# One GRU's gates, blend and norm scale split into pieces and dealt out over attention tiles

## The reference

```
x = x + gnn(layernorm(x), adj)      # sum of two GRU cells, weighted with diag(adj)
x = x + ffn(layernorm(x))           # 8 experts, top 2 by a router, hidden width 341

gnn:  node_support = adj0 @ h                          # adj0: adj without its diagonal
      edge_output  = gru(node_support, h, edge weights)
      edge_support = mean over 3 heads of (softmax(e + mask) * adj0) @ (h @ W)
      node_output  = gru(edge_support, h, node weights)
gru:  r, z = sigmoid(gi_r + gh_r), sigmoid(gi_z + gh_z);  n = tanh(gi_n + r * gh_n)
      out  = (1 - z) * n + z * h
```

## Time and profile before

| | us |
|---|---|
| median of 3 runs | 486.14 (484.26 to 486.72) |
| profiled execution, its own time | 485.43 |
| its span, first to last instruction | 483.7 |
| around the span | 1.73 |
| mean granted TensorE clock | 0.982 |
| PE busy | 427.7 |
| DVE busy | 333.4 |

### The profile page before, as it was taken

The page is one execution under the profiler, slowest core; times in us unless marked ns, Lnnn a source line. Parts: engine busy times, 40 slices in busy tenths (PEclk is TensorE's granted clock), DMA queues, the critical chain, the costliest instruction groups (busy, mean ns, idle before and its releaser), DMA issues.

```text
span 483.7 us, 6133 instructions
## 1 busy us (share of the span) xinstructions
PE 427.7 (88%) x1768; PEld 247.7 (51%) x1768; DVE 333.4 (69%) x719; ACT 233.4 (48%) x377; POOL 63.8 (13%) x112
## 2 busy tenths in 40 slices
PE   3678798998989999999989999999988889899996
PEld 1533454454646654545534343444444446668785
DVE  0997999989576742325873888696767946775574
ACT  4998999887995523013243022233123026544331
POOL 5000000000110000000000000100420412464433
PEclk9769999999999999998999999999999999999999
DMA  8898700000001000000000001360100012023142
GB/s 283 237 335 315 294 0 0 1 0 1 3 0 57 1 1 1 0 0 2 1 1 0 1 0 33 108 201 22 41 22 0 30 48 64 28 59 86 49 131 63
DMA packets 25356, 30.45 MB, mean 63 GB/s; under 512 B 3266, under 2 KB 19855, under 8 KB 25319
## 3 DMA queue, kind: packets, MB, share of 16 engines
q1 hardware_dynamic: 22711, 26.56, 17.0%
q0 software_dynamic: 1568, 2.92, 1.7%
q10 hardware_dynamic: 1040, 0.52, 0.4%
HBM read 19.73 MB, written 10.26 MB: 62 GB/s over the span
## 4 chain that ended last, share of the span: by engine, by line
PE 48%; DVE 26%; ACT 11%; issue 10%; POOL 3%; DMA 1%; SPq 0%; DVEq 0%; POOLq 0%; ACTq 0%
PE bank L1371 8%; PE bank L1185 5%; DVE pr_ring L2141 4%; PE bank L1450 4%; PE bank L1434 3%; PE bank L1435 3%; DVE t_units L1584 3%; PE bank L1319 2%; PE bank L1144 2%; PE bank L1265 2%; DVE y_units L1578 2%; PE bank L1360 2%; ACT hr_ring L824 2%; PE bank L1441 2%; PE bank L1266 2%
## 5 line engine op out<-in xcount | busy, mean ns | idle before, releaser
L1371 PE MATMUL bank<-pr_ring,hW 128*128 128x512 f32 (+3 forms) x198 | 93.8, 558 | 9.2 <-DVE pr_ring L2141 8.2
L2141 DVE SCALAR_TENSOR_TENSOR pr_ring<-adjT,regR,bank 128x512 f32<-128x512 f32 (+3 forms) x99 | 63.9, 680 | 27.5 <-PE bank L1360 26.1
L1371 PEld LDWEIGHTS bank<-pr_ring,hW 128*128 128x128 f32 (+1 forms) x198 | 33.4, 190 | 42.6 <-DVE pr_ring L2141 28.4
L1144 PE MATMUL bank<-hr_ring,W2s 128*128 128x512 f32 (+1 forms) x96 | 43.9, 544 | 0.0
L1945 DVE TENSOR_TENSOR hr_ring<-hr_ring,bank 128x512 f32<-128x512 f32 (+1 forms) x48 | 29.5, 619 | 16.2 <-ACT hr_ring L824 9.5
L1033 PE MATMUL bank<-y_units,msg 128*128 128x512 f32 (+3 forms) x66 | 30.4, 584 | 11.0 <-DVE y_units L1599 10.9
L999 PE MATMUL bank<-zhi,W1hi 128*128 128x512 f32 (+1 forms) x48 | 32.4, 675 | 1.8 <-ACT hr_ring L824 1.6
L824 ACT ACTIVATE hr_ring<-bank,b1c 128x512 f32<-128x512 f32 (+1 forms) x48 | 30.0, 626 | 7.2 <-PE bank L1001 7.2
L603 POOL DMA_INDIRECT xg<-rowx,slot x22 | 22.2, 1008 | 65.3 <-DVE slot L1702 58.7
L609 POOL DMA_INDIRECT yg<-pr_ring,goes x23 | 22.1, 960 | 42.3 <-DVE pr_ring L2170 41.4
L2181 DVE TENSOR_TENSOR hbuf<-hbuf,bank 128x341 f32<-128x341 f32 x30 | 15.2, 507 | 16.0 <-PE bank L1435 13.9
(11 more groups left out here) (351 smaller groups left out, 859.0 us busy)
## 6 DMA issues: line engine op xcount, KB each, us to landing
xg<-zeros SPq DMA_DIRECT2D x1, 6110.0 KB
wall<-in_w SPq DMA_DIRECT2D x2, 1364.0 KB
adjT<-in_adjT SPq DMA_DIRECT2D x1, 2560.0 KB
xblk<-xg SPq DMA_DIRECT2D x30, 65.0 KB, 1.8
adjT<-in_adjT SPq DMA_DIRECT2D x1, 1650.0 KB
adjT<-in_adjT SPq DMA_DIRECT2D x3, 512.0 KB, 5.9
adjT<-in_adjT SPq DMA_DIRECT2D x1, 1024.0 KB
W1f<-in_W SPq DMA_DIRECT2D x1, 1024.0 KB, 12.4
```

What stands on the lines that cost most here:

```text
L1144: nc.tensor.matmul(B_Y0[:, 0:w], W2s[:, e, m, :], hr_ring[:, q % RING0, 0:w], start=False, stop=(e == E - 1 and m == M0 - 1)).then_inc(s[" ...
L1371: nc.tensor.matmul(B_ACC[:, 0:w], hW[0:r, j, k * P:(k + 1) * P], ring[0:r, 0:w], start=(k == 0 and j == 0), stop=(k == K - 1 and j == T - ...
L2141: nc.vector.scalar_tensor_tensor(out=pr_ring[0:r, 4 + p % R_RING, 0:w], in0=adjT[0:r, j, cols(c)], scalar=g_col[0:r, j, k:k + 1], in1=B_F[ ...
```

## The change

The five products of the node GRU's gates for chunk 1 no longer stand together behind step (6, 0). The two from the state are issued first, behind steps (5, 7) and (5, 9); they wait only for things that are old by then (the weights, x of the chunk before, the copied tokens of chunk 0). The three from the support are issued behind (6, 0), (6, 1) and (6, 2). The three operations of the blend stand behind numerators (6, 8), (6, 9) and (6, 10) in place of all behind (6, 7), and the three of the norm scale behind (7, 5), (7, 6) and (7, 7) in place of all behind (7, 4). Everything else that comes behind them moves by one to three steps. ACT's order is the same. No instruction is added or removed.

```diff
 MAIN_PE
-    (5, 4): [("prefix", 0)], (6, 0): [("gates", 1, 1)], (6, 2): [("mid", 1, 1)], (6, 9): [("mean", 3, 1)],
-    (7, 0): [("var", 3, 1)], (7, 5): [("logits", 4), ("ztok", 1)], (7, 9): [("prefix", 1)]}
+    (5, 4): [("prefix", 0)], (5, 7): [("state", 1, 0)], (5, 9): [("state", 1, 1)], (6, 0): [("support", 1, 0)], (6, 1): [("support", 1, 1)],
+    (6, 2): [("support", 1, 2)], (6, 4): [("mid", 1, 1)], (7, 0): [("mean", 3, 1)],
+    (7, 2): [("var", 3, 1)], (7, 7): [("logits", 4), ("ztok", 1)], (8, 0): [("prefix", 1)]}
 MAIN_DVE
-    (6, 5): [("mid", 1, 1)], (6, 7): [("blend", 1, 1)], (6, 9): [("add", 1, 1)], (7, 4): [("scale", 3, 1)],
-    (7, 7): [("scores", 4), ("ranks", 4), ("picks", 4)], (7, 9): [("weights", 4)], (8, 0): [("slots", 4)], (8, 4): [("starts", 0)], (8, 6): [("starts", 1)],
+    (6, 6): [("mid", 1, 1)], (6, 8): [("blend", 1, 1, 0)], (6, 9): [("blend", 1, 1, 1)], (6, 10): [("blend", 1, 1, 2)], (7, 0): [("add", 1, 1)],
+    (7, 5): [("scale", 3, 1, 0)], (7, 6): [("scale", 3, 1, 1)], (7, 7): [("scale", 3, 1, 2)],
+    (7, 9): [("scores", 4), ("ranks", 4), ("picks", 4)], (8, 0): [("weights", 4)], (8, 2): [("slots", 4)], (8, 6): [("starts", 0)], (8, 8): [("starts", 1)],
     (8, 10): [("starts", 2), ("list", 0)]}

+            def gate_of_state(c, i):
+
+                at(pe, "gru_in", 112 + 32)
+                at(pe, "x3_ready", c)
+                at(pe, "htok_set", C + c)
+                nc.tensor.matmul(GRU_BANK[1][c][i][:, 0:width(c)], gruw[:, 1, i * P:(i + 1) * P], zT[:, cols(c)], start=True, stop=False)
+
+            def gate_of_support(c, i):
+
+                at(pe, "es_set", c + 1)
+                mm = nc.tensor.matmul(GRU_BANK[1][c][i][:, 0:width(c)], gruw[:, 0, i * P:(i + 1) * P], ES[c][:, 0:width(c)], start=(i == 2), stop=True)
+                if i == 2:
+                    mm.then_inc(s["gru_ps"], 1)
```

More of the change, by code:

```diff
@@ L1291, in gat_side @@
                     gates(*task[1:])
+                elif task[0] == "state":
+                    gate_of_state(*task[1:])
+                elif task[0] == "support":
+                    gate_of_support(*task[1:])
                 elif task[0] == "mid":
@@ L1552, in ln_center, with ln_scale, ln_scale_first, ln_scale_second @@
                 nc.vector.tensor_tensor(ln_buffers(l, c)[0], xT[:, cols(c)], ln_bank(l, c)[:, 0:w], ALU.subtract).then_inc(s["ln_xc"], 1)
-            def ln_scale(l, c):
+            def ln_scale(l, c, part=None):
                 n, w = LN_AT[l, c], width(c)
                 xc, y, v = ln_buffers(l, c)
+                if part in (None, 0):
+                    ln_scale_first(l, c, n, w, xc, y)
+                if part in (None, 1):
+                    ln_scale_second(l, c, n, w, v)
+                if part in (None, 2):
+                    ln_scale_third(l, c, n, w, xc, v)
+            def ln_scale_first(l, c, n, w, xc, y):
                 at(dve, "ln_y0", n + 1)
                 nc.vector.scalar_tensor_tensor(out=xc, in0=center_bank(l)[:, 0:w] if centred(l, c) else xc, scalar=-0.5, in1=y, op0=ALU.mult, op1=ALU.mult).then_inc(s["ln_step"], 1)
+            def ln_scale_second(l, c, n, w, v):
                 at(dve, "ln_y2", n + 1)
@@ L1562, in ln_scale, with ln_scale_third @@
                                                op1=ALU.mult).then_inc(s["ln_step"], 1)
+            def ln_scale_third(l, c, n, w, xc, v):
                 at(dve, "ln_step", 2 * n + 2)
@@ L2027, in mid, with blend @@
                 nc.vector.tensor_tensor(a, a, b_ni[:, 0:w], ALU.add).then_inc(s["gru_a"], 1)
-            def blend(n, c):
+            def blend(n, c, part=None):
                 g, w = n * C + c, width(c)
@@ L2033, in blend @@
                 at(dve, "gru_n", g + 1)
-                link(nc.vector.tensor_tensor(d, zT[:, cols(c)], a, ALU.subtract))
-                link(nc.vector.scalar_tensor_tensor(out=d, in0=tz, scalar=1.0, in1=d, op0=ALU.add, op1=ALU.mult))
-                link(nc.vector.scalar_tensor_tensor(out=d, in0=d, scalar=0.5, in1=a, op0=ALU.mult, op1=ALU.add))
+                if part in (None, 0):
+                    link(nc.vector.tensor_tensor(d, zT[:, cols(c)], a, ALU.subtract))
+                if part in (None, 1):
+                    link(nc.vector.scalar_tensor_tensor(out=d, in0=tz, scalar=1.0, in1=d, op0=ALU.add, op1=ALU.mult))
+                if part in (None, 2):
+                    link(nc.vector.scalar_tensor_tensor(out=d, in0=d, scalar=0.5, in1=a, op0=ALU.mult, op1=ALU.add))
             def add(n, c):
```

## The result

The changed kernel takes 487.58 us (median of 20 runs, 486.50 to 492.28) against 485.49 us (20 runs, 484.08 to 487.34) before: a ratio of 1.0051, 95% interval 1.0036 to 1.0067, so 2.5 us slower (the two medians alone are 2.1 apart). A run more than 1.5% above the fastest of its kernel is left out of the ratios: one of 493.46 us in the experiment with the slots as early as they go, and one of 517.01 us in the one with only the wait longer. The profiled execution took 486.50 us with a span of 484.8 us; before it was 485.43 and 483.7.

The account below looks back on a forecast made before the run. POOL's scatters and the block load bound the experts' start. Shifts 1.72 - 0.30 + 0.47 + 0.01 + 0.75 - 1.07 = +1.58 us, on the four-run mean 485.64, gave 487.2, range 484.9 to 489.2.

Parts of the forecast that it names:

- one rival, priced but held unlikely: Wait ahead of block 0: TensorE's clock falls to 1.2 GHz, costing 1.2 us on top of 1.58, 488.4 us; chance 0.13.
- three signs of being wrong: Slots at or before 378.34; PE's queue, not the load, ending the wait before block 0; a 0.50 window behind 394 us.
- What bounds the kernel: End of attention: POOL's eight scatters, then block 1's load, set the first expert product; scatters have no slack.
- Head 5 and the gates: Two state products put 1.72 us on PE ahead of head 6; the sixth product and `mid` come +1.42.
- Blend and add: Chunk 1 after `mid`: three numerators instead of two between blend's start and add, so x of the chunk comes +1.89.
- It saves nothing: Dealing blend replaces PE's one 1.45 us wait by four, about 1.8 us in all; DVE is late by the same work.
- Scale, logits, slots: Head 7 on: third scale operation +2.65; logits start directly behind PE's next attend, +1.58; slots, scatters and load all +1.58.
- The clock: PE idles some 1.7 us ahead of block 0; the clock could fall by the skill's rule, need not by the windows.
- The faster rival: Dealing frees DVE's 4.43 us idle ahead of 354.77; less two steps of 0.70, -3.0 us, 482.6; chance 0.11.
- the delay would be hidden: No-effect rival at the scatters: their delay is hidden, only PE's 0.33 us shows, 486.0 us; chance 0.10.

## Why the prediction was right

The forecast was 487.2 us and within 484.9 to 489.2; it is 487.58. The ratio puts the loss at 2.5 us, where the sum said 1.58. The difference is one rival, priced but held unlikely. So the mechanism was right up to the start of the experts and wrong behind it, and that the time still came out within 0.4 us of the forecast is in part luck: about 1 us is missing from the sum, and the two medians lie closer together than the ratio. The range went up to 489.2 and so held the rival's 488.4 too. The chances fare less well: a change within 0.5% had 0.65 and a slower one 0.25, and the measured 0.51% lies on that border, with an interval that leaves out no change.

Of the three signs of being wrong that the prediction names, two did not come (the slots are not earlier, and the load, not PE's queue, ended the wait) and the third did: behind 394 us the windows show 0.58 and 0.56, and those of 1 us from 397 to 399 show 0.50.

**What bounds the kernel:** right. The scatters' last landing set the start of the experts before and after, and moving the slots alone moved it (slots +1.14, start +1.09).

**Head 5 and the gates:** right in size (+1.73 for 1.72, +1.40 for 1.42). As a cause it was read too simply: with the gates together again only 0.30 us came back. In that one execution the state products in head 5 account for 0.30 of the 1.55 us at the slots, while the sixth product stands behind (6, 4).

**Blend and add:** the shift is right (+1.88 for +1.89). "It saves nothing" was wrong in one respect: the pieces keep PE's waits short. With blend in one piece behind the later `mid` the wait was 2.09 us and the clock fell, which took the delay from +1.34 at x of the chunk to +2.63 at the slots. That is one profile of each; that the pieces are what kept the clock up is likely and not shown.

**Scale, logits, slots:** +2.63, +1.56 and +1.55, for 2.65, 1.58 and 1.58. That the logits take back most of it is confirmed by the scale alone, +0.16 at the slots. The forecast of the change as a sum of shifts was good to 0.04 us at every step up to the slots, and the first expert product is +1.51 for +1.58.

**The clock:** this is the term that failed. I gave its fall 0.13, because the stretch from 394 us had kept 1.00 with PE busy 0.81 of 2.00 us. It fell, and the price I took from the slow pair of the earlier trace rows, 1.2 us, is near the 1.0 measured (1.06 came back when the wait was filled). That the wait ahead of block 0 causes it is shown from both sides: filled, it does not fall; made longer in the kernel before, it does. All six profiles that had PE idle there for 0.82 us or more show it, and none of the six with 0.53 us or less. The Trainium skill (TensorE: Matmul & The Clock Gate, What's actually happening) says that the clock goes by how busy the engine has been recently; the trace agrees (PE was busy 0.63 of 2.00 us in 394 to 396, and the clock is 0.58 behind it), and the page's rule was the better guide here than the single row that I set against it. The likeliest case should have been the 1.58 and the clock together, a shift of 2.8 us by my own figures, for 2.5 measured.

**The faster rival**, that DVE's idle 4.43 us come free, is out: with the gates alone nothing came earlier. That the delay would be hidden is out by the slots alone.

Open is how much of each run's spread is the clock. Only profiled executions show where it fell; the changed kernel's two slowest runs, at 492.3 us, have a mean clock of 0.965 against 0.979, and where they lost it was not seen.

Another part of the spread can lie in the last blocks. The profiles of the seventeen idle products and of only the slots later are the slowest runs of their sets (490.85 and 491.9 us). In them an operation of DVE on `own` took 2.35 and 2.31 us where the kernel before has 0.16, and the `joiner` behind it 2.59 and 2.58 where most take 0.42; PE then waited 2.44 and 2.40 us, and the span ended some 3 us later behind the last expert product than in the other ten. In the twelve profiles 20 `joiner` operations took over 1 us, and each of them ended 0.21 to 0.23 us behind an operation of POOL (of 1.0 or 2.4 us) that ran beside it. An edit that shifts DVE against POOL there can add to a timed difference or take from it, and no run here holds that fixed. The timeline of DVE and POOL with seventeen idle products:

```profile
474.20 2.35 POOL L637 TENSOR_TENSOR answer<-x3tok,picked_y 128x1024 f32<-128x1024 f32 x1 [1.77 <-DMA picked_y<-yg]
474.22 2.35 DVE L2192 TENSOR_TENSOR own<-xblk,own 128x1 f32<-128x1 f32 x1
...
476.61 2.59 DVE L2193 TENSOR_SCALAR joiner<-place_id,own 128x384 f32<-128x384 f32 x1
```

The 2.5 us of the timed runs thus agree with the 2.52 us of the profiles in size, and the split into 1.5 and 1.0 is shown for the profiles only.

## What to carry to other kernels

When work is dealt out over a loop, follow it to the thing that leaves the loop last, here eight scatters of 1.26 us each that start when the last small vector operation is done: splitting an operation gains nothing if its last piece comes later. Count the steps between producer and consumer on both queues, since the logits regained 1.1 us merely by standing right behind what they wait for. And every us that is saved or lost ahead of a wait of TensorE changes the length of that wait: fill it with idle products up to the expected end of the wait, and look at the granted clock behind it in the profile.

## What was not expected of the hardware

The wait ahead of the first block and what the clock did behind it, in the twelve profiled executions: 0.23, 0.46 and 0.53 us, and none in three more (one of them with 0.80 ahead of the second block): 1.00; 0.82 with 0.85 ahead of the second block, 1.73, 1.74, 1.75, 1.76 and 1.94 us: down to 1.2 GHz for 3 to 7 us. Elsewhere length decides less. Inside the attention a wait of 1.45 us for a numerator kept 1.00 in all eight profiles that have it, and one of 1.23 us in all five, while the one of 1.18 us in the experiment with the early slots and the one of 2.09 us in the one with only the gates were followed by 1.2 GHz. At 216 us (up to 220 in the later ones) the same wait of 1.19 us, between 1.18 and 1.29, was followed by 1.2 GHz in four of the twelve profiles, that of the kernel before among them, and by 2.4 GHz in eight, that of the changed kernel among them. So such a wait can go either way from execution to execution, and one profile does not tell which.

Behind the wait ahead of block 0 a stretch at 1.2 GHz cost less than half its length at the last expert product: some 3.4 us cost 0.7 to 1.3 (four profiles; the changed kernel's 1.0), and some 6.8 us cost 1.8 and 1.85 (two profiles). That other engines bound part of the stretch is the likely reason, not a shown one.
